# Attention tiles and feed-forward rounds of six layers: two stages per layer, or one stream

## The chip, the core and the metric

The kernel runs on one core of one Trainium2 chip. The metric is the device time of one execution in microseconds (us). Five engines work beside each other and meet at semaphores: TensorE (matmuls and transposes; PE in the profile, its weight loads PEld), VectorE (DVE), ScalarE (ACT), GpSimd (POOL) and SyncE (SP), which starts the transfers. Every engine has its instructions in order in a queue of its own.

## The reference, cut to what matters

64 sequences of 64 tokens, 128 features, in fp32. A cross-attention comes first and a second cross-attention and a mixture of experts come last; between them, and only this is changed, stand six layers of local attention and a gated feed-forward block:

```
for l in range(6):
    x = x + attn(shift_tokens(x), Wqkv[l], Wo[l])      # 16 heads of 64, window 32
    x = x + ffn(shift_tokens(x), W1[l], W2[l])         # 128 -> 2 x 341 -> 128

attn:  q, k, v = split(x @ Wqkv);  q, k = rotary(l2norm(q)), rotary(l2norm(k))
       softmax(8 q k^T, masked) @ v @ Wo
ffn:   xn = layernorm(x) * g + b;  a, gate = split(xn @ W1 + b1)
       (a * gelu(gate)) @ W2 + b2
```

`shift_tokens` moves half of the features by one token, so a tile is read again through a transfer within the core's memory, from `Y` to `xsd` (attention) or `xsf` (feed-forward).

## The kernel before

The residual `Y` holds 32 tiles of 128 tokens (NT). A layer's attention works tile by tile. A feed-forward round takes two tiles, so there are 16 rounds (NF). Every engine runs through the same steps with a body of its own, and the order within the body is written by hand. In a step of the attention (`d_body`) four tiles are in flight: `n` is loaded and turned, `a` is projected (`chunk`, `values`) and gets its rotary embedding (`rope`, the squares and their sums), `b` is turned again (`turn`), gets its scores and the softmax, `c` gets its probabilities turned (`probsT`), the product with the values (`pv`) and the output projection into bank `pp`, which VectorE adds to `Y`. GpSimd sums the rope's halves (`turn_sum`), scales by the inverse norm (`unit`) and the softmax's inverse sum (`probs`). A round (`f_body`) has stages of the same kind: statistics, normalise and turn (`xnT`), three hidden blocks (`hidden`, ScalarE's `gelu`, VectorE's `gated`), and the down product (`f_y`) with its sum.

`stream` (L305 to L319) makes the loop: some steps written out, a loop of two steps, L313, and the last steps written out. It is called twice per layer, with 35 steps for the attention and 19 for the rounds. Around it every engine loops over the layers (L1557 on TensorE, L1117 on VectorE):

```
with pe.Fori(0, DEPTH) as l:
    ...
    stream(pe, NT, d_body, l * NT, l * (NT // 2), 4)
    pe.wait_ge(sem("ffn_loaded"), l * FFN_LOADS + FFN_LOADS)
    ...
    stream(pe, NF, f_body, l * NF, l * (NF // 2), 4)
```

Names used below: turn bank (`pt_`, named turn in the profile), rope on VectorE is L987 and L988, its idle time is seen at L987; L999 is the clamp of the squared norms, L1436 a projection chunk, L1454 a turn of `b`, L1481 of the probabilities, L1511 of the next tile's input, L1495 `pv`, L1524 the output projection; L1535 a hidden block, L1547 the down product; L760 the gelu, L772 the explicit load of the exponential's table; L743 the logarithm of the norms. The last layer's rounds hold two further stages (`e_`, `h`), the norm for the next cross-attention. SyncE's queue issues the tile loads, the round loads and the weights in one order; `past(engine, name, count)` is a wait on a counter.

## Time and profile before

| what | us |
|---|---|
| median of 3 runs | 4562.96 (4555.24 to 4566.67) |
| the profiled execution, its own time | 4562.57 |
| its span, first to last instruction | 4560.5 |
| TensorE busy | 4214.2 (92%) |
| VectorE busy | 3501.8 (77%) |
| GpSimd busy | 2884.7 (63%) |
| ScalarE busy | 2547.9 (56%) |
| first layer's first turn, TensorE | at 687.93 |
| last layer's last down product, TensorE | at 3924.17 |

The mean granted TensorE clock is 0.961 of full speed. The profile is of one execution; "start" is counted from the span's start. Matmuls are pipelined, their ends are modelled, so the distance from one start to the next says more than a duration.

### The profile page before, as it was taken

How to read it: one execution, taken by the hardware profiler on the slowest of the kernel's cores; microseconds unless marked ns; L12 is line 12 of the kernel's file. 1: busy time of each engine (PE TensorE's matmuls, PEld its weight loads, DVE VectorE, ACT ScalarE, POOL GpSimd, SP SyncE). 2: the span in 40 equal slices, each digit the busy share in tenths (PEclk: the TensorE clock that was granted, in tenths of full speed). 3: DMA queues.
4: the chain of work that ended last, by engine and by line, in shares of the span. 5: the costliest groups of instructions: out<-in, count | busy, mean ns of one | idle time of the engine just before them, and what ended most of it. 6: DMA issues, size and time to landing. Idle time of an engine off the chain costs nothing.

```text
span 4560.5 us, 148424 instructions
## 1 busy us (share of the span) xinstructions
PE 4214.2 (92%) x51751; PEld 2907.5 (64%) x51751; DVE 3501.8 (77%) x7368; ACT 2547.9 (56%) x5842; POOL 2884.7 (63%) x3664
## 2 busy tenths in 40 slices
PE   6999998999899988999889998999889998788899
PEld 4777775666666666666656666666666665566655
DVE  4666668997699967999679985999769995577566
ACT  2555555666466655666456663666546664355322
POOL 2333337887288855888378882888648885655300
PEclk9999999999999999999999998999999999887699
DMA  2000010000100010000100001000000000000000
GB/s 83 7 7 7 6 41 6 5 5 6 43 6 5 5 30 20 5 5 6 36 11 5 5 6 43 6 5 5 28 22 5 5 7 11 21 12 12 4 7 11
DMA packets 160438, 64.07 MB, mean 14 GB/s; under 512 B 121365, under 2 KB 155937, under 8 KB 159521
## 3 DMA queue, kind: packets, MB, share of 16 engines
q1 hardware_dynamic: 160288, 62.05, 5.3%
q8 instruction: 98, 1.61, 0.1%
q14 instruction: 52, 0.42, 0.0%
HBM read 26.54 MB, written 2.10 MB: 6 GB/s over the span
## 4 chain that ended last, share of the span: by engine, by line
PE 33%; DVE 29%; issue 25%; POOL 5%; ACT 4%; DVEq 1%; SPq 1%; ACTq 1%; POOLq 0%; DMA 0%
DVE ss L993 6%; DVE big L988 6%; DVE mx L1005 5%; PE pj L1535 3%; DVE big L987 3%; DVE e L1012 3%; DVE qn L987 3%; PE pj L1378 3%; PE turn L1454 3%; PE pp L1336 2%; PE sc L1547 2%; ACT big L698 2%; PE po L1351 2%; PE sc L1697 1%; PE turn L1535 1%
## 5 line engine op out<-in xcount | busy, mean ns | idle before, releaser
L1436 PE MATMUL pj<-wqkv,xcT 128*128 128x512 f32 x1536 | 830.4, 624 | 24.5 <-DVE big L988 9.6
L690 ACT ACTIVATE big<-pj 128x512 f32<-128x512 f32 x768 | 459.1, 598 | 244.3 <-PE pj L1436 176.1
L530 POOL TENSOR_TENSOR big<-big 128x512 f32<-128x512 f32 x384 | 486.0, 1277 | 132.0 <-DVE big L988 132.0
L988 DVE TENSOR_TENSOR big<-pj,ropes 128x512 f32<-128x512 f32 x768 | 522.4, 680 | 0.0
L530 POOL TENSOR_TENSOR qn<-qn,big 128x512 f32<-128x512 f32 x384 | 486.5, 1278 | 35.6 <-DVE big L988 35.6
L993 DVE TENSOR_REDUCE ss<-big 128x8 f32<-128x512 f32 x768 | 504.2, 678 | 0.1
L1524 PEld LDWEIGHTS pp<-wo,oT 128*128 128x128 f32 x3072 | 366.8, 196 | 154.5 <-ACT oT L713 154.1
L525 POOL TENSOR_TENSOR e<-e,rc 128x512 f32<-128x512 f32 x384 | 392.8, 1045 | 46.1 <-DVE rc L1023 46.1
L1524 PE MATMUL pp<-wo,oT 128*128 128x128 f32 x3072 | 403.9, 286 | 7.0 <-ACT oT L713 7.0
L519 POOL TENSOR_TENSOR qn<-qn,ny 128x512 f32<-128x512 f32 x384 | 396.9, 1045 | 7.5
L519 POOL TENSOR_TENSOR big<-big,ny 128x512 f32<-128x512 f32 x384 | 396.8, 1045 | 7.5
L725 ACT ACTIVATE e<-e 128x512 f32<-128x512 f32 x384 | 242.1, 630 | 280.1 <-DVE e L1012 280.1
L1443 PE MATMUL pj<-wqkv,xcT 128*64 128x512 f32 x1536 | 375.5, 606 | 18.1 <-DVE big L988 18.0
L987 DVE TENSOR_TENSOR qn<-pj,ropec 128x512 f32<-128x512 f32 x384 | 262.5, 683 | 105.9 <-PE turn L1454 86.1
L987 DVE TENSOR_TENSOR big<-pj,ropec 128x512 f32<-128x512 f32 x384 | 262.6, 684 | 87.2 <-PE turn L1454 69.9
L1454 PEld LDWEIGHTS turn<-K,qn 128*128 128x128 f32 x1536 | 179.1, 140 | 217.0 <-POOL qn L519 109.8
L1454 PEld LDWEIGHTS turn<-K,big 128*128 128x128 f32 x1536 | 182.0, 141 | 206.9 <-POOL big L519 95.6
L1012 DVE TENSOR_TENSOR e<-sc,mx 128x512 f32<-128x512 f32 x384 | 265.7, 692 | 46.5
L1005 DVE TENSOR_REDUCE mx<-sc 128x8 f32<-128x512 f32 x384 | 260.6, 679 | 44.9 <-PE sc L1470 44.9
L1436 PEld LDWEIGHTS pj<-wqkv,xcT 128*128 128x128 f32 x1536 | 235.1, 193 | 93.0 <-DVE big L988 75.8
L1454 PE MATMUL turn<-K,qn 128*128 128x128 f32 x1536 | 234.2, 275 | 39.5 <-ACT big L698 23.8
L1481 PEld LDWEIGHTS pp<-K,e 128*128 128x128 f32 x1536 | 187.6, 143 | 122.9 <-issue 96.8
(322 smaller groups left out, 9605.8 us busy)
## 6 DMA issues: line engine op xcount, KB each, us to landing
wqkv<-in_L_ffn_Wqkv SPq DMA_DIRECT2D x6, 1536.0 KB, 6.5
xsd<-Y SPq DMA_DIRECT2D x192, 32.0 KB
xsd<-Y SPq DMA_DIRECT2D x384, 15.8 KB
xsf<-Y SPq DMA_DIRECT2D x96, 64.0 KB
xsf<-Y SPq DMA_DIRECT2D x192, 31.5 KB
xsx<-Y SPq DMA_DIRECT2D x64, 64.0 KB, 1.8
xsx<-CT SPq DMA_DIRECT2D x64, 64.0 KB, 1.9
wo<-in_L_ffn_Wo SPq DMA_DIRECT2D x6, 512.0 KB, 7.5
```

Source lines behind the costliest of these rows:

```text
L519: nc.gpsimd.tensor_tensor(uv, uv, bc(ny[:, tile.par, 8 * i:8 * i + 8], DK), ALU.mult).then_inc(sem("d_un"), 1)
L525: nc.gpsimd.tensor_tensor(ev, ev, bc(rc[:, p, 0:8], S), ALU.mult).then_inc(sem("d_pr"), 1)
L530: nc.gpsimd.tensor_tensor(U[a.par][i], U[a.par][i], t2b[i % 2], ALU.add).then_inc(sem("d_add"), 1)
L690: nc.scalar.activation(sqb[i % 2], pj[i % 2][:, :], ACT.Square).then_inc(sem("d_sq"), 1)
L987: nc.vector.tensor_tensor(t1v, pv, cos, ALU.mult)
L988: nc.vector.tensor_tensor(t2v, swapped, sin, ALU.mult).then_inc(sem("d_r"), 1)
L993: nc.vector.tensor_reduce(ss[:, i, :], sqb[i % 2].rearrange("p (h d) -> p h d", d=DK), AX, ALU.add).then_inc(sem("d_ss"), 1)
L1005: nc.vector.tensor_reduce(mx[:, p, 0:8], sv, AX, ALU.max).then_inc(sem("d_mx"), 1)
L1012: nc.vector.tensor_tensor(e[:, p, :].rearrange("p (a t) -> p a t", t=S), sv, bc(mx[:, p, 0:8], S), ALU.subtract).then_inc(sem("d_sub"), 1)
L1436: mm(pj[i % 2][:, :], xcT[:, a.par, :], wqkv[:, i * 512:i * 512 + 512], start=True, stop=True).then_inc(sem("d_ch"), 1)
L1454: last = nc.tensor.transpose(pt_[:, j * P:j * P + P], U[b.par][i][:, j * P:j * P + P], ident)
L1524: last = mm(pp[:, 0:D], oT[:, k, :], wo[:, k, :], start=(k == 0), stop=(k == HP - 1))
```

## The change

All engines go through one list of steps, 192 tiles of all six layers and eight steps behind them, made by `all_layers`. A `Pass` gives the body the tiles `n`, `a`, `b`, `c` and the rounds that are in flight; round r stands two steps for each of its stages, so that one round is begun in every second step. Even steps do the hidden blocks, odd ones the normalisation and, one stage later, the down product. The first eight steps of a layer are written out, the others are a loop of four. The hidden blocks now use the banks `po` of the attention output, the down product uses `pp`, and the turns of `b` use `pt_` and `pp` in turn. The weights of a layer are loaded in parts (`q`, `scales`, `k`, `v`, `o`; `norm`, `up`, `biases`, `down`), each behind the last use of the old part. ScalarE loads the gelu's table and then the exponential's in every even step. Its square of a chunk stands ahead of the first copy; the clamp is now two activations and an identity on it. The last layer's additional norm lies in the last layer's steps. The core of the diff:

```diff
-f_hid = [pj[0], pj[1], pt_]
+f_hid = [po[0], po[1], po[0]]
+f_hidden = sb("f_hidden", [P, 3, FT * P])
+f_xcT = sb("f_xcT", [P, 2, FT * P])
+LAGS, ROUND_LAGS, SEAM = 4, 5, 8
+def all_layers(eng, body):
+tiles, rounds = DEPTH * NT, DEPTH * NF
+def known(k, **more):
+    def one(j, n, m):
+        return Tile(j, j % m, j % 2, j // 2) if 0 <= j < n else None
+    body(Pass([one(k - i, tiles, NT) for i in range(LAGS)], [one(k // 2 - i, rounds, NF) for i in range(ROUND_LAGS)],
+              k % 2, in_po=min(max(k - 3, 0), tiles), **more))
+def moving(l, p, i, **more):
+    def one(j, m, k):
+        return Tile(l * m + j + k * i, (j + k * i) if p < NT else j % m, j % 2, l * (m // 2) + (j // 2) + (k // 2) * i)
+    c = one(p - 3, NT, 4)
+    body(Pass([one(p - q, NT, 4) for q in range(LAGS)], [one(p // 2 - q, NF, 2) for q in range(ROUND_LAGS)],
+              p % 2, in_po=c.g, **more))
+def inside(l, last):
+    with eng.Fori(0, (NT - SEAM) // 4) as i:
+        for p in range(SEAM, SEAM + 4):
+            moving(l, p, i, last=last)
+for k in range(SEAM):
+    known(k, at=k, layer=0)
+with eng.Fori(0, DEPTH - 1) as l:
+    inside(l, False)
+    for p in range(SEAM):
+        moving(l, NT + p, 0, at=p, layer=l + 1)
+inside(DEPTH - 1, True)
+for k in range(tiles, tiles + SEAM):
+    known(k, last=True)
+def attention_weights(l, part):
+    if part == "q":
+        past(sp, "d_ch", l * (4 * NT) - 2)
+        past_waits(sp, "went_on")
+        sp.dma_start(wqkv[:, 0:INNER], Wqkv[l, :, 0:INNER]).then_inc(sem("wq_in"), 16)
+    if part == "k":
+        past(sp, "d_ch", l * (4 * NT))
+        past_waits(sp, "went_on")
+        sp.dma_start(wqkv[:, INNER:2 * INNER], Wqkv[l, :, INNER:2 * INNER]).then_inc(sem("wk_in"), 16)
+    if part == "v":
+        past(sp, "d_vp", l * (2 * NT))
...
+def load_steps(p):
+    if p.at == 0:
+        tile_load(p.n)
+        if isinstance(p.layer, int):
+            for part in ("norm", "up", "biases", "down"):
+                ffn_weights(0, part)
+            past(sp, "x_ch", 6 * NT)
+            for wst, src in ((wst1, w1), (wst3, w3), (wst2, w2)):
+                sp.dma_start(wst, src.rearrange("e i d -> i e d")).then_inc(sem("exp_loaded"), 16)
+        else:
+            for part in ("q", "scales", "k", "v"):
+                attention_weights(p.layer, part)
+    elif p.at == 6 and not isinstance(p.layer, int):
+        ffn_weights(p.layer, "down")
+        tile_load(p.n)
+    else:
+        tile_load(p.n)
+    if not isinstance(p.layer, int):
+        if p.at == 3:
+            attention_weights(p.layer, "o")
+        if p.at == 4:
+            ffn_weights(p.layer, "norm")
+            ffn_weights(p.layer, "up")
+            ffn_weights(p.layer, "biases")
+    if p.odd_round(2):
+        ffn_round(p.odd_round(2).g, p.odd_round(2).t, p.odd_round(2).par)
+all_layers(sp, load_steps)
     unit(b, 1)
     probs(0)
+    unit(b, 2)
...
     turn_sum(0)
+    mean_square(p.odd_round(2))
+    if z:
+        past(pool, "z_x", z.t * 2 + 1)
+        nc.gpsimd.tensor_tensor(X[:, rows, :], Y[:, rows, :], X[:, rows, :], ALU.add).then_inc(sem("z_x"), 1)
     turn_sum(1)
+    inverse_deviation(p.odd_round(2))
+    z = p.odd_round(4) if p.last else None
+    if z:
+        past(pool, "norm_ag", z.t + (NT + 1))
+        rsqrt(0, FT, "norm_nr", z.t * 2 + 2 * NT)
     turn_sum(2)
+    turn_sum(3)
...
+    if r:
+        nc.scalar.preload_act_table_set("gelu_and_others")
+    square(0)
     turned(0)
-    square(0)
+    gelu(0)
     turned(1)
     square(1)
-    probsT(0)
     if n:
         past(act, "d_xT", n.g + 1)
         past(act, "d_vp", n.g * 2 - 2)
         nc.scalar.copy(xcT[:, n.par, :], pt_[:, 0:P]).then_inc(sem("d_xc"), 1)
+    gelu(1)
+    probsT(0)
     square(2)
+    gelu(2)
+    probsT(1)
     turned(2)
-    probsT(1)
     square(3)
     turned(3)
+    if r or p.begins(0):
+        nc.scalar.preload_act_table_set("natural_log_exp_and_others")
     if a:
-        past(act, "d_cl", a.g + 1)
-        nc.scalar.activation(xh[:, :], ssc[:, :], ACT.Ln).then_inc(sem("d_ln"), 1)
+        past(act, "d_ss", a.g * 4 + 4)
+        nc.scalar.activation(xr[:, :], ss[:, :, :].rearrange("p c h -> p (c h)"), ACT.Relu, bias=tiny[:, 1:2]).then_inc(sem("d_cl"), 1)
+        past(act, "d_cl", a.g * 2 + 1)
+        nc.scalar.activation(xh[:, :], xr[:, :], ACT.Ln, bias=tiny[:, 0:1]).then_inc(sem("d_ln"), 1)
+    outT(0)
+    if a:
+        past(act, "d_nt", a.g * 4)
+        nc.scalar.activation(ssc[:, :], xr[:, :], ACT.Identity, bias=tiny[:, 0:1]).then_inc(sem("d_cl"), 1)
         past(act, "d_ln", a.g + 1)
         past(act, "d_un", a.g * 4 - 4)
         nc.scalar.activation(ny[:, a.par, :], xh[:, :], ACT.Exp, scale=-0.5).then_inc(sem("d_rn"), 1)
-    outT(0)
     outT(1)
+    x = p.odd_round(2)
+        nc.scalar.activation(f_xcT[:, x.par, :], pt_[:, 0:2 * P], ACT.Identity, scale=fg[:, 0:1], bias=fg[:, 1:2]).then_inc(sem("f_xT"), 1)
     exps(0)
     values(0)
     exps(1)
     values(1)
+    def gated(j):
+        if h:
+            if j == 0 and p.begins(6):
+                dve.wait_ge(sem("up_in"), p.layer * 112 + 112)
+            m = FBLK[j][1]
+            past(dve, "f_gl", h.g * 3 + (j + 1))
+            if j == 0:
+                past(dve, "f_y", h.g - 1)
+            nc.vector.scalar_tensor_tensor(hT[0:m, h.par, j, :], f_hid[j][0:m, 256:512], fb1[0:m, 0, j:j + 1], f_hidden[0:m, j, :], ALU.add, ALU.mult).then_inc(sem("f_hT"), 1)
     rope(0)
     square_sum(0)
...
+    gated(0)
     rope(1)
...
     square_sum(1)
+    gated(1)
...
     square_sum(2)
+    gated(2)
...
     rope(2)
     square_sum(3)
-    clamp()
     rope(3)
...
+    y = p.odd_round(3)
+    if y:
+        past(dve, "f_y", y.g + 1)
+        ds = bass.ds(y.t * FT, FT)
+        nc.vector.tensor_tensor(Y[:, ds, :], pp[:, 0:2 * D].rearrange("p (a d) -> p a d", a=2), Y[:, ds, :], ALU.add).then_inc(sem("y_ready"), FT)
     row_max(0)
+            if i == 0:
+                past(pe, "d_tc", b.g * 4 - 1)
+                if p.rounds[3] and not p.odd:
+                    past(pe, "f_xT", p.rounds[3].g + 1)
+            elif i == 1:
+                past(pe, "d_res", b.g - 1)
+            elif i == 2:
+                if n:
+                    past(pe, "d_xc", n.g + 1)
+                else:
+                    past(pe, "d_tc", b.g * 4 + 1)
+            elif c:
+                past(pe, "d_pc", c.g * 2 + 2)
             else:
-                past(pe, "d_tc", b.g * 4 + i)
+                past(pe, "d_tc", b.g * 4 + 2)
+            bank = (pt_, pp)[i % 2]
+    def hidden(j):
+        if h:
+            o, m = FBLK[j]
+            if j == 0:
+                past(pe, "f_xT", h.g + 1)
+                if p.begins(6):
+                    pe.wait_ge(sem("up_in"), p.layer * 112 + 112)
+            if j < 2:
+                past(pe, "d_oc", p.in_po * 2 + (j - 1))
+            else:
+                past(pe, "f_hT", h.g * 3 + 1)
+            for k in (1, 0):
+                last = mm(f_hid[j][0:m, (1 - k) * 256:(1 - k) * 256 + 256], fw1[:, k * FI + o:k * FI + o + m], f_xcT[:, h.par, :], start=True, stop=True)
+            last.then_inc(sem("f_h"), 1)
+    chunk(0)
+    hidden(0)
     turn(0)
-    chunk(0)
     turn(1)
     chunk(1)
-    probsT(0)
+    hidden(1)
     if n:
         pe.wait_ge(sem("d_in%d" % n.par), n.half * 48 + 48)
         if b:
-            past(pe, "d_tc", b.g * 4 + 2)
+            past(pe, "d_tc", b.g * 4 + 1)
         else:
             past(pe, "d_xc", n.g)
         nc.tensor.transpose(pt_[:, 0:P], xsd[:, n.par, :], ident).then_inc(sem("d_xT"), 1)
+    probsT(0)
     chunk(2)
     turn(2)
+    hidden(2)
     probsT(1)
     chunk(3)
     turn(3)
     pv()
     scores()
+    if y:
+        past(pe, "f_hT", y.g * 3 + 3)
+        if p.begins(7):
+            pe.wait_ge(sem("fw2_in"), p.layer * 48 + 48)
+        if b:
+            past(pe, "d_tc", b.g * 4 + 4)
+        elif c:
+            past(pe, "d_pc", c.g * 2 + 2)
+        else:
+            past(pe, "d_res", p.in_po)
+            pe.wait_ge(sem("y_ready"), y.g * FT + NT)
+        for i in range(FT):
+            for j, (o, m) in enumerate(FBLK):
+                k = m + (j == 2)
+                last = mm(pp[:, i * D:i * D + D], hT[0:k, y.par, j, i * P:i * P + P], fw2[0:k, j, :], start=(j == 0), stop=(j == 2))
+        last.then_inc(sem("f_y"), 1)
...
     values(0)
+    if x:
...
     values(1)
     if c:
+        if p.begins(3):
+            pe.wait_ge(sem("wo_in"), p.layer * 16 + 16)
         past(pe, "d_oc", c.g * 2 + 2)
+        if b:
+            past(pe, "d_tc", b.g * 4 + 4)
+        else:
+            past(pe, "d_pc", c.g * 2 + 2)
+        if y:
+            pe.wait_ge(sem("y_ready"), y.g * FT + (NT + FT))
         for k in range(HP):
```

## Rows read from the trace of the kernel before

**Rows 1.** Windows by stage: length, busy us (instructions) per engine, clock, DMA.
```profile
741.00:1104.00 363.00, 356.75 (x5057) 231.37 (x5054) 331.70 (x596) 247.89 (x514) 324.40 (x380) 1.00 0.02 5
...
687.90:1143.80 455.90, 431.63 (x5984) 278.16 (x5984) 392.89 (x709) 294.68 (x608) 383.66 (x448) 0.98 0.02 5
1143.80:1224.80 81.00, 72.87 (x416) 59.82 (x416) 47.68 (x177) 34.10 (x66) 14.23 (x32) 0.94 0.21 56
```

**Rows 2.** Timeline of TensorE, steady attention step: start, us, engine, line, operation.
```profile
918.10 1.02 PE L1436 MATMUL pj<-wqkv,xcT 128*128 128x512 f32 x2
919.28 0.63 PE L1454 MATMUL turn<-K,big 128*128 128x128 f32 x4 [0.15 <-ACT big L698]
919.75 1.02 PE L1436 MATMUL pj<-wqkv,xcT 128*128 128x512 f32 x2
920.61 0.60 PE L1481 MATMUL pp<-K,e 128*128 128x128 f32 x4
921.04 0.27 PE L1511 MATMUL turn<-K,xsd 128*128 128x128 f32 x1
921.39 1.13 PE L1436 MATMUL pj<-wqkv,xcT 128*128 128x512 f32 x2
922.35 0.60 PE L1454 MATMUL turn<-K,big 128*128 128x128 f32 x4
...
924.14 0.60 PE L1454 MATMUL turn<-K,big 128*128 128x128 f32 x4
924.67 1.30 PE L1495 MATMUL po<-pT,xo 64*64 64x64 f32 x64
...
929.19 2.05 PE L1524 MATMUL pp<-wo,oT 128*128 128x128 f32 x16
...
931.51 1.02 PE L1436 MATMUL pj<-wqkv,xcT 128*128 128x512 f32 x2
```

**Rows 3.** Timeline of TensorE, one steady feed-forward round.
```profile
1188.00 1.03 PE L1535 MATMUL turn<-kT,fw 128*85 128x256 f32 x4
...
1190.82 1.50 PE L1547 MATMUL sc<-fw,hT 128*128 128x128 f32 x12
...
1192.38 1.02 PE L1535 MATMUL turn<-kT,fw 128*85 128x256 f32 x4
```

**Rows 4.** Groups of instructions, steady attention: busy us, mean ns, idle before.
```profile
L530 POOL TENSOR_TENSOR big<-big 128x512 f32<-128x512 f32 x55 | 69.6, 1277 | 3.7 <-DVE big L988 3.7
...
L999 DVE TENSOR_TENSOR ssc<-ss,tiny 128x32 f32<-128x32 f32 x27 | 20.8, 771 | 0.9
...
L743 ACT ACTIVATE xh<-ssc 128x32 f32<-128x32 f32 x27 | 6.2, 229 | 41.1 <-DVE ssc L999 41.1
```

**Rows 5.** Groups of instructions, steady feed-forward.
```profile
L1060 DVE SCALAR_TENSOR_TENSOR hT<-pj,fb,e 128x256 f32<-128x256 f32 x30 | 13.8, 477 | 2.6 <-ACT e L760 2.5
```

**Rows 6.** Timeline of VectorE, the first rope of a step.
```profile
906.64 0.69 DVE L987 TENSOR_TENSOR big<-pj,ropec 128x512 f32<-128x512 f32 x1 [0.84 <-PE turn L1454]
```

**Rows 7.** Timeline of ScalarE, the two table loads of a layer.
```profile
1150.77 1.28 ACT L760 ACT_TABLE_LOAD   x1 [2.30 <-PE pj L1535]
1152.07 0.90 ACT L760 ACTIVATE e<-pj,fb 128x256 f32<-128x256 f32 x2
...
1219.61 0.47 ACT L760 ACTIVATE e<-turn,fb 85x256 f32<-85x256 f32 x1 [1.73 <-PE turn L1535]
1220.10 1.28 ACT L772 ACT_TABLE_LOAD   x1
```

**Rows 8.** TensorE's branches by source line: layer loop, then step loops (ns min/median/max).
```profile
L1557 PEldq COMPARE_BRANCH  x6: 76/3403/3602, 1220.9 to 3924.3; - x6
...
L313 PEldq COMPARE_BRANCH  x141: 76/208/242, 109.8 to 4267.6; - x141
```

**Rows 9.** Timeline of TensorE, fourth tile's turn and the last down product.
```profile
719.94 0.27 PE L1511 MATMUL turn<-K,xsd 128*128 128x128 f32 x1
...
3924.17 1.60 PE L1547 MATMUL sc<-fw,hT 128*128 128x128 f32 x12 [1.23 <-DVE hT L1060]
```

## What the change does to the time, predicted before its run

> **What bounds the kernel now.** I read the busy shares by stage first. In the steady part of an attention stage TensorE is busy 356.75 of 363 us, VectorE 331.70, GpSimd 324.40, ScalarE 247.89, at a granted clock of 1.00 [rows 1]. A step is 13.41 us long (projection of one tile at 918.10, of the next at 931.51 [rows 2]), so per step VectorE has 12.25 us of work, GpSimd 11.98, ScalarE 9.16. Busy matmuls can hide waits, so I then read the order of TensorE inside one step, start to start [rows 2]. A projection chunk that is not held takes 0.86 (919.75 to 920.61), four transposes 0.43 (920.61 to 921.04). Against that, chunk 0 is followed after 1.18 (0.32 lost: the second turn waits until ScalarE has emptied the only turn bank), the transpose of the next tile's input by 0.35 instead of about 0.11 (0.24 lost, chunk 2 waits for the first rope), chunk 2 takes 0.96 (0.10 lost) and the last turn 0.53 (0.10 lost). That is 0.76 lost, 12.65 of work: TensorE is the bound and little is idle.
>
> A feed-forward round is 4.38 us (1188.00 to 1192.38 [rows 3]), TensorE without a gap: hidden blocks 2.82, down product and turn 1.56. The stage as a whole, 81.0 us [rows 1], is 16 x 4.38 = 70.1 and 10.9 of filling and draining.
>
> The idle time lies at the ends. An attention stage lasts 455.9 us [rows 1]. Its first three steps take 32.0 (687.9 to the fourth tile's turn at 719.94 [rows 9]), then 29 steps of 13.41 are 388.9, and 35.0 are left for the last two and a half steps. With 32 x 13.41 = 429.1 of steady time, 26.8 are ends; with the 10.9 of the feed-forward stage 37.7 per layer, 226 us in six. The last layer's feed-forward stage holds the next stage's statistics besides and is longer; the sum below takes that in by its end.
>
> **The change, part by part.**
>
> *One stream.* There are 192 tiles and 5 + 3 steps behind them, and 96 rounds at one per two steps. Let P be the length of a pair of steps. TensorE's work in a pair is 2 x 12.65 + 4.38 = 29.7 with no wait left; with the waits of now it is 2 x 13.41 + 4.38 = 31.2. Both ends go into the range. The other engines in a pair: VectorE 24.5, less two clamps of 0.77 [rows 4], plus 47.68 / 16 = 2.98 of a round = 25.9; ScalarE 18.3 + 34.10 / 16 = 2.13 + two table loads of 1.28 (under 0.1 of which the round already holds) + four activations on 32 columns of 0.23 = 23.8; GpSimd 24.0 + 0.89 = 24.9 [rows 1, 4, 7]. None reaches 29.7, so the bound stays TensorE as long as no chain through two or three engines is longer.
>
> *Order and banks.* Turns alternate between two banks, which takes away the 0.32. Chunk 0 comes before turn 0, and its square before ScalarE's first copy. VectorE now sits idle 0.84 before its first rope [rows 6], because that square is behind a copy; the first rope comes earlier by up to about this, and the 0.24 ahead of chunk 2 and its own 0.10 can go. In the even step a hidden block lies between chunk 0 and turn 0 and covers GpSimd's last scaling too. The clamp leaves VectorE (0.77 [rows 4]) for two more small activations on ScalarE. GpSimd's fourth sum moves ahead of the Newton step, so turn 0's operand comes later by 1.28 [rows 4]; chunk 0 (0.86) and in even steps hidden 0 (a third of 2.82) now lie ahead of that turn, so I count nothing in even steps and up to 0.4 in odd ones.
>
> *Table loads.* A load takes 1.28 (from 1150.77), starts 0.02 behind the activation before it (1219.61 + 0.47, load at 1220.10), and the gelu starts 0.02 behind it [rows 7]. Two of them stand in each even step. The first lies where ScalarE ends the tile before and TensorE does chunk 0 and hidden 0 (0.86 + 0.94), so it is nearly hidden; it costs between 0 and 1.28. The second lies between the last turn's copy and the copies of the attention output, which the output projection waits for. TensorE has the product with the values, the scores and the values' projection to do meanwhile (4.5 us, 924.67 to 929.19 [rows 2]), so I leave 0.3 of it on the path; the bounds are again 0 and 1.28.
>
> The Trainium skill, "ScalarE: Activation LUTs", section "What ACT_TABLE_LOAD costs", adds a drain of 1.38 us to every switch. The trace shows no such gap on either side of the load. By that rule P would be up to 2.8 longer, 33.1, and the time about 4565; what rows give for it is rival E.
>
> *P.* Best 29.7; I give back 0.3 for the second load and 0.3 for GpSimd's later scaling and the first load together: P = 30.3.
>
> *Start and end.* From 687.9 the first three steps stay 32.0; steps 3 and 4 have no round work, 26.8; steps 5 to 191 are 93.5 pairs; the rest of step 192, then 193 and 194, are the 35.0 of now plus two hidden groups and one down group, 2 x 2.82 + 1.56, 42.2. Then the last round runs alone: the latency of a round is the 10.9 of the stage's ends plus one period of 4.4; its input is now loaded only when the last tile is done, about 2 more (estimate), 17.4 in all. Together 806.3 + 93.5 P. The statistics for the next stage lie inside the stream; behind the last down product comes what comes now.
>
> *Seams.* Five times the layer's weights change in mid stream. SyncE's queue is in order: the value weights wait for the last values of the old layer, and behind them stand the second tile's input and a round's input; chunk 2 needs the value part as well as the key part. I count 2 us for that, 0 to 5. The loop over layers still jumps back five times: TensorE's jump takes 3.4 us (L1557), against 0.2 for a loop over steps (L313) [rows 8]. That jump is in the 37.7 of now and comes back here with 3.4. Five seams of 5.4 are 27.
>
> *Sum.* The last down product starts at 3924.17 and ends at 3925.8 [rows 9]. New: 806.3 + 93.5 x 30.3 + 27 = 3666.4. That is 259.4 earlier; against the profiled execution's 4562.57 us (span 4560.5) it gives 4303, and the median of the three runs, 4562.96, is only 0.4 away. I say 4300.
>
> **The rivals.**
>
> *A. The waits stay* (P = 31.2). For: every step now has 0.76 of waits although each engine has slack, so a ring through ScalarE and VectorE sets them, and ScalarE gets 5.5 us more per pair. Against: the two largest have named causes that the new order removes. 806.3 + 2917.2 + 27 = 3750.5, so 4387.
>
> *B. The loop over steps becomes a far jump.* It goes from two steps to four. TensorE issues 187 matmuls and 187 weight loads a step (5057 in 27 steps [rows 1]) and some 20 queue instructions (estimate); four steps with two rounds are about 1700 instructions. The jump over a layer, about 3600, costs 3.4 us; the jump over two steps, about 800, costs 0.2 [rows 8]. 1700 lies between. There are 30 such jumps (six rounds in six layers, the last of each not taken): 30 x 3.4, less what TensorE's queue covers, is 75 to 102; with 87 it gives 4390.
>
> The Trainium skill, "Runtime: NRT & Kernel Launch", section "Instruction fetch mechanics", gives TensorE room for 2048 instructions and a fetch for a taken branch that leaves it. By that the new loop fits, narrowly, and B costs nothing; a whole layer does not fit, and there the trace agrees.
>
> *C. All waits go* (P = 29.7): 4247. It needs both table loads hidden and is not likely.
>
> *D. Slower: ScalarE's additions stand in series with its waits.* Place: the even step. ScalarE waits 4.2 of 13.41 us now for partners. If those waits stay and loads, gelus and small activations (2.56 + 1.42 + 0.45) are added behind them, the even step is 17.8, and the odd one 13.41 + 1.56 + 0.45 = 15.4, P = 33.3, 4584. The deciding point is P = (3925.8 - 833.3) / 93.5 = 33.1. For: hidden 2 waits for the first gated block, and the probabilities' product waits for the last, so matmul, gelu and gate follow each other twice in the step. Against: three hidden blocks give ScalarE and VectorE 2.8 us of TensorE time to use, and one gelu takes 0.47, one gated block 0.48 [rows 5, 7].
>
> *E. The table loads stand on the path in full.* A load finds ScalarE idle in most places now; behind a busy engine it could cost twice its 1.28. Two in a pair, 2.56 beyond the 0.6 that I count: P = 32.9, 4547. Against it speaks the load at 1220.10, which follows a gelu at once [rows 7]. The Trainium skill's drain, above, is this rival.
>
> *F. It doesn't overlap.* A round could run as an island, if a barrier held the tiles. The waits in the step are per tile and round, none on a whole layer, so this gets no chance of its own.
>
> **How the numbers follow.** Forecast 0.50; A 0.20; B 0.16; C 0.06; D 0.04; E 0.04, half of it so far that nothing measurable is left. The range for 8 in 10 goes from between C and below it (waits under 0.76 may be uncounted) to above A and B, with a small part of both together: 4210 to 4430. A change of 0.3%, 14 us, is about what a measurement of this kernel can tell. Faster is all but D and half of E, 0.94; within 0.02; slower 0.04.
>
> **What the changed profile would show.** The granted clock stays 1.00 from the fourth step to the last tile, and the forty slices show no dips between layers. Starts of chunk 0 two steps apart give P: 30.3 if I am right, 31.2 for A. A branch of 3.4 us on the step loop's line is B. Turn 1 follows turn 0 by 0.43 without waiting for a copy; VectorE's idle time before the first rope falls below 0.84. VectorE's share rises towards 85% and ScalarE's to 78% in the steady part. Around each layer change at most 6 us are lost. I am wrong if TensorE waits over 1.5 us per pair for ScalarE's output copies (A or D), if the seams take over 10 us each, or if TensorE is not the engine with the least idle time.

## The result, and the profile after

| | us | ratio to before, 95% interval |
|---|---|---|
| before, median of 4 runs beside the new kernel | 4561.01 | |
| after, median of 4 runs | 4435.03 (4433.17 to 4438.25) | 0.9725 (0.9708 to 0.9741) |
| forecast | 4300, 4210 to 4430 | |

The change makes the kernel faster by 126 us, where I had forecast 260. The measured time lies 5 us above my range.

Page of the kernel after: the engines' busy time, the queue that brings instructions (packets, MB, share), and the chain that ended last.

```profile
PE 4164.6 (94%) x51751; PEld 2901.7 (65%) x51751; DVE 3525.9 (80%) x7208; ACT 2841.5 (64%) x6406; POOL 2869.7 (65%) x3633
...
q8 instruction: 393, 6.44, 0.6%
...
PE 77%; DVE 9%; issue 8%; POOL 3%; ACT 1%; SPq 1%; DVEq 0%; ACTq 0%; POOLq 0%; DMA 0%
```

TensorE is still the bound, but 8% of the chain is "issue": TensorE waited for nothing that the profile shows. The instruction queue moved 393 packets; in the kernel before it had moved 98 (1.61 MB).

The stretch that answers to the steady window of [rows 1], with the same columns:

```profile
757.00:1192.00 435.00, 420.70 (x5414) 285.82 (x5413) 372.94 (x719) 321.36 (x655) 338.00 (x407) 0.99 0.06 14
```

TensorE is idle in 14.3 of 435 us although the two kinds of work are interleaved now. Where those are is seen at the turn of the next tile's input, one per step. Timeline of TensorE, kernel after:

```profile
822.54 0.27 PE L1649 MATMUL turn<-K,xsd 128*128 128x128 f32 x1
...
836.17 0.27 PE L1649 MATMUL turn<-K,xsd 128*128 128x128 f32 x1
...
847.20 2.05 PE L1697 MATMUL pp<-wo,oT 128*128 128x128 f32 x16
851.25 1.12 PE L1542 MATMUL pj<-wqkv,xcT 128*128 128x512 f32 x2 [2.00 <-issue]
...
855.67 0.27 PE L1649 MATMUL turn<-K,xsd 128*128 128x128 f32 x1
```

From one such turn to the next is 13.63 us in every second step (822.54 to 836.17) and 16.80 in the others where nothing disturbs it, a pair 30.43. From 836.17 to 855.67 it is 19.50: 2.00 idle ahead of chunk 0 at 851.25. That idle time comes once in four steps, at the loop's end. Branches of TensorE's sequencer by source line (ns, min/median/max): the loop over steps (L360) and over layers (L366).

```profile
L360 PEldq COMPARE_BRANCH  x36: 83/3626/3983, 847.3 to 3752.5; - x36
```
```profile
L366 PEldq COMPARE_BRANCH  x5: 79/3532/3732, 1299.8 to 3377.2; - x5
```

Each of these lines also counts the last pass, where the branch is not taken (83 and 79 ns): of the 36 on L360 30 are taken, of the 5 on L366 four. In [rows 8] the loops over two steps had 208 ns. The other engines' branches on L360 have medians of 45 to 56 ns. Now the loop's end, on TensorE alone, costs as much as a layer's.

I added up, over the 186 distances from the sixth tile's turn (744.56) to the last one's (3741.69), what each is above 16.80 or 13.63. The sum is 167.1 us:

| place | us |
|---|---|
| end of the 4-step loop and the step behind (27 of 30 branches slow) | 110.8 |
| layer jump and the step behind (4, 18.6), and the same two steps in the first and the last layer (1.7) | 20.3 |
| first three steps of a layer, the seam (5) | 32.8 |
| exit of the 4-step loop, all else | 3.2 |

The 27 are all 25 in layers 0 to 4 and two of the last layer's five.

A part of this is TensorE's clock. Behind some of the gaps it falls to its lower level, 1.2 GHz. Timeline of TensorE at the loop's next end, then windows behind three gaps (2.00, 2.21 and, at the seam below, 3.36 us idle), with the columns of [rows 1]:

```profile
915.61 1.67 PE L1542 MATMUL pj<-wqkv,xcT 128*128 128x512 f32 x2 [2.21 <-issue]
```
```profile
851.25:854.65 3.40, 3.40 (x16) 2.45 (x17) 1.36 (x3) 1.47 (x4) 1.95 (x2) 1.00 0.02 5
916.10:919.40 3.30, 3.30 (x9) 2.17 (x8) 1.20 (x2) 0.60 (x1) 1.69 (x2) 0.50 0.02 5
1195.95:1199.35 3.40, 3.40 (x11) 2.26 (x11) 3.40 (x11) 0.60 (x1) 1.11 (x1) 0.50 0.11 24
```

The step of a slow loop end is 2.4 to 3.0 us too long where the clock stays at 1.00 (18 of the 27) and 4.1 to 4.6 where it falls (9). It also falls in the step of the tables at all five seams, and behind three of the four layer jumps. In the whole stream 64.8 us stand at 0.50, so up to 32 of the 167.1 us (estimate, half of that) are the price of the clock behind a gap and not of the gap itself.

The seam. Timelines of the kernel after, first TensorE, then VectorE, then GpSimd:

```profile
1191.53 0.31 PE L1649 MATMUL turn<-K,xsd 128*128 128x128 f32 x1
1191.78 0.63 PE L1601 MATMUL pp<-K,e 128*128 128x128 f32 x4
1195.76 1.94 PE L1542 MATMUL pj<-wqkv,xcT 128*128 128x512 f32 x2 [3.36 <-DVE big L1108]
```
```profile
1190.41 0.39 DVE L1088 SCALAR_TENSOR_TENSOR ropec<-K,qs 128x64 f32<-128x64 f32 x1 [0.16 <-issue]
1190.72 1.05 DVE L1089 SCALAR_TENSOR_TENSOR ropes<-K,qs 128x32 f32<-128x32 f32 x1
1191.68 1.08 DVE L1090 SCALAR_TENSOR_TENSOR ropes<-K,qs 128x32 f32<-128x32 f32 x1
1192.69 1.11 DVE L1088 SCALAR_TENSOR_TENSOR ropec<-K,qs 128x64 f32<-128x64 f32 x1
1193.72 0.18 DVE L1089 SCALAR_TENSOR_TENSOR ropes<-K,qs 128x32 f32<-128x32 f32 x1
1193.82 0.18 DVE L1090 SCALAR_TENSOR_TENSOR ropes<-K,qs 128x32 f32<-128x32 f32 x1
1194.42 0.69 DVE L1107 TENSOR_TENSOR big<-pj,ropec 128x512 f32<-128x512 f32 x1 [0.42 <-DVE ropes L1090]
```
```profile
1189.67 1.05 POOL L627 TENSOR_TENSOR e<-e,rc 128x512 f32<-128x512 f32 x1
1190.67 1.04 POOL L621 TENSOR_TENSOR qn<-qn,ny 128x512 f32<-128x512 f32 x1
1191.67 1.05 POOL L627 TENSOR_TENSOR e<-e,rc 128x512 f32<-128x512 f32 x1
1192.67 1.04 POOL L621 TENSOR_TENSOR qn<-qn,ny 128x512 f32<-128x512 f32 x1
```

Before the first rope of a new layer VectorE builds six small tables, 3.6 us in a row. TensorE's chunk 2 waits 3.36 for the rope behind them, and the chunk then takes 1.94 instead of 1.02, at the granted clock of 0.50 shown above. The old kernel has the same six instructions, but at the start of a layer, where the pipeline was filling anyway. I had not priced them.

ScalarE's two table loads, groups of the kernel after (busy us, mean ns, idle before):

```profile
L858 ACT ACT_TABLE_LOAD x97 | 124.5, 1283 | 1.7
L839 ACT ACT_TABLE_LOAD x96 | 123.2, 1283 | 8.9 <-issue 7.3
```

193 loads with 10.6 us of idle time ahead of them in all: there is no drain on entering a load. Behind it there is none either: the median distance from a load's end to the next activation's start is 0.01 us.

The end of the stream, and the first turn of the last part:

```profile
3741.69 0.27 PE L1649 MATMUL turn<-K,xsd 128*128 128x128 f32 x1
...
3808.46 1.60 PE L1673 MATMUL pp<-fw,hT 128*128 128x128 f32 x12 [1.07 <-DVE hT L1148]
...
3818.24 0.41 PE L1734 MATMUL pj<-K,xsx 128*128 128x128 f32 x2 [0.30 <-ACT egT L947]
```

The last down product ends at 3810.06, before at 3925.77 [rows 9]: 115.7 earlier. The span is 4431.3, so 621.2 follow, where 634.7 followed before; those 13.5 make the 129.2 by which the span is shorter.

### The profile page after: what moved, and what is told of

Its sections match the earlier page's. It is cut to its first block, busy times and chain, and to the rows that moved or that the text cites. A ratio compares the mean times of both kernels' runs of the same rounds, so it can differ in the third digit from the quotient of the medians.

```text
span 4431.3 us, 147857 instructions
## 1 busy us (share of the span) xinstructions
PE 4164.6 (94%) x51751; PEld 2901.7 (65%) x51751; DVE 3525.9 (80%) x7208; ACT 2841.5 (64%) x6406; POOL 2869.7 (65%) x3633
## 4 chain that ended last, share of the span: by engine, by line
PE 77%; DVE 9%; issue 8%; POOL 3%; ACT 1%; SPq 1%; DVEq 0%; ACTq 0%; POOLq 0%; DMA 0%
PE pj L1542 13%; PE pp L1697 7%; PE pj L1549 7%; PE po L1634 6%; PE po L1617 4%; PE sc L1588 4%; PE pp L1572 4%; PE turn L1572 3%; PE pp L1601 3%; PE pj L1480 3%; PE pp L1438 2%; PE pp L1673 2%; DVE big L1108 2%; PE po L1453 2%; PE sc L1832 2%
## 5 line engine op out<-in xcount | busy, mean ns | idle before, releaser
L1542 PE MATMUL pj<-wqkv,xcT 128*128 128x512 f32 x1536 | 817.2, 614 | 86.9 <-issue 66.3
L1114 DVE TENSOR_REDUCE ss<-big 128x8 f32<-128x512 f32 x768 | 515.5, 672 | 4.4 <-ACT big L793 4.4
L1697 PEld LDWEIGHTS pp<-wo,oT 128*128 128x128 f32 x3072 | 357.3, 191 | 156.1 <-issue 109.4
L1549 PE MATMUL pj<-wqkv,xcT 128*64 128x512 f32 x1536 | 394.4, 613 | 1.3 <-DVE big L1108 1.3
L1697 PE MATMUL pp<-wo,oT 128*128 128x128 f32 x3072 | 393.9, 281 | 1.6 <-ACT oT L816 1.2
L1634 PE MATMUL po<-f_xcT,fw 128*128 128x256 f32 (+1 forms) x1152 | 307.0, 391 | 1.5 <-DVE hT L1148 0.8
L1634 PEld LDWEIGHTS po<-f_xcT,fw 128*128 128x128 f32 (+1 forms) x1152 | 208.1, 185 | 121.2 <-issue 95.4
L1588 PE MATMUL sc<-kT,big 64*64 64x64 f32 x12288 | 234.2, 222 | 27.2 <-issue 27.1
L1132 DVE TENSOR_REDUCE sm<-e 128x8 f32<-128x512 f32 x384 | 259.4, 676 | 0.0
```

The costliest lines, as they stand in the source:

```text
L1114: nc.vector.tensor_reduce(ss[:, i, :], sqb[i % 2].rearrange("p (h d) -> p h d", d=DK), AX, ALU.add).then_inc(sem("d_ss"), 1)
L1542: mm(pj[i % 2][:, :], xcT[:, a.par, :], wqkv[:, i * 512:i * 512 + 512], start=True, stop=True).then_inc(sem("d_ch"), 1)
L1549: last = mm(pj[bb][a2 * 64:a2 * 64 + 64, :].rearrange("p (q c) -> p q c", c=2 * DK), xcT[:, a.par, bb * 64:bb * 64 + 64], wv[:, a2], start ...
L1588: last = mm(sc[q, c0:c0 + S], qT[r, hp, q], kT[r, hp, q], start=False, stop=True, skip_group_check=True)
L1634: last = mm(f_hid[j][0:m, (1 - k) * 256:(1 - k) * 256 + 256], fw1[:, k * FI + o:k * FI + o + m], f_xcT[:, h.par, :], start=True, stop=True)
L1697: last = mm(pp[:, 0:D], oT[:, k, :], wo[:, k, :], start=(k == 0), stop=(k == HP - 1))
```

## The experiments

Theory T1: TensorE's backward branch of the 4-step loop has to fetch its target again, because the loop (1701 instructions by my count of the generated ones and by the profile's records from one branch to the next, against 792 for two steps before) with what is fetched ahead needs more room than there is. T2: the loop's end costs that for another reason (register work, waits that meet, the other engines' loops, the clock). S1 and S2 are the two theories of the seam: the build of the tables lies on the path, or the weights arrive late. A slow branch is one of over 3 us; "increments" are idle semaphore instructions that only move the code behind them. Four runs stand behind each median up to e8, five behind e9, one behind e10 to e14, so these five have no interval; e1 to e4, e5 to e8, e9 to e11 and e12 to e14 ran together, each group beside the kernel before (4556.5, 4562.6, 4558.1, 4565.1 us).

| run | us | ratio to before (95%) | slow branches of 30 |
|---|---|---|---|
| e1 | 4357.8 | 0.9568 (0.9547 to 0.9590) | 8 |
| e2 | 4420.8 | 0.9700 (0.9677 to 0.9723) | 30 |
| e3 | 4337.9 | 0.9522 (0.9495 to 0.9550) | no loop |
| e4 | 4413.3 | 0.9695 (0.9668 to 0.9721) | 27 |
| e5 | 4413.3 | 0.9677 (0.9649 to 0.9705) | 27 |
| e6 | 4346.0 | 0.9526 (0.9499 to 0.9552) | no loop |
| e7 | 4323.6 | 0.9484 (0.9460 to 0.9507) | 0 |
| e8 | 4324.8 | 0.9496 (0.9470 to 0.9522) | no loop |
| e9 | 4309.5 | 0.9453 (0.9430 to 0.9476) | 0 |
| e10 | 4332.3 | | 0 |
| e11 | 4339.6 | | 5 |
| e12 | 4442.3 | | 30 |
| e13 | 4370.1 | | 5 |
| e14 | 4292.2 | | 0 |

**Padding, e1 and e2.** The only edit, in TensorE's program ahead of its first wait for data:

```
+            for _ in range(190):            # e2: 40
+                past_waits(pe, "went_on")
             pe.wait_ge(s_ld, NLOAD)
```

> 190 idle semaphore increments are put into TensorE's program at its very start, where it waits for the first loads; nothing else changes. Counted in instructions of 64 bytes, TensorE's 4-step loop is 1701 long, or 6.6 blocks of 256 instructions (the instruction queue moves 16 KB at a time). In the changed kernel it lies over 8 such blocks in layers 0 to 4 (22.4 to 29.1), where each of the 25 backward branches measured 3.6 us, and over 7 in the last layer (42.35 to 49.0), where only 2 of 5 did. The padding moves both loops to start just behind a block's edge (23.2 to 29.8 and 43.1 to 49.7), 7 blocks each. Theory T1 (the backward branch has to fetch its target again because the loop with the block fetched ahead needs more room than there is): the slow branches go in all six layers, or in 3 of 5 as in the last: 60 to 110 us less, 4325 to 4375 us. Rival T2 (the 3.6 us is the price of the loop's end itself: register work, waits that meet there, other engines' loops, the clock): the place of the code can't matter, 4430 to 4440 us. The padding's own cost is nothing under either.

> The same padding with 40 increments: the loop of layers 0 to 4 stays over 8 blocks (22.6 to 29.2), the last layer's, so far over 7, now lies over 8 (42.5 to 49.2). T1: the last layer's five branches all become slow, three more than before, each about 4 us with the step after it: 10 to 16 us more, 4445 to 4451 us. T2: 4430 to 4440 us.

Branches of the 4-step loop, first of e1, then of e2; and the instruction queue of each:

```profile
L360 PEldq COMPARE_BRANCH  x36: 76/222/4023, 843.5 to 3667.4; - x36
```
```profile
L360 PEldq COMPARE_BRANCH  x36: 83/3388/3928, 849.2 to 3742.5; - x36
```
```profile
q8 instruction: 223, 3.65, 0.3%
```
```profile
q8 instruction: 420, 6.88, 0.6%
```

The same instructions at another place take 77 us less. The median branch falls from 3626 to 222 ns and 170 fewer packets of instructions are moved. T2, by which the place doesn't matter, is out, and the clock with it: it falls behind a gap and is not what makes the gap. e2 came as T1 says in number (the last layer's five are all slow), but not in time: 14 us less, not 10 to 16 more. Its 30 slow ends cost 107.0 with the steps behind, 3.6 each, where the 27 before cost 4.1 each; the step behind is longer by 1.0 on average in the kernel after, and in e2 only in the last layer, by 0.8. Why it is longer stays open. So the price of a slow jump moves with the place too, and I had taken it for fixed.

**TensorE's loops written out, e3 and e6.** e3 replaces the loop over steps, e6 all loops of the stream, on TensorE alone (`for i in range(6)` for `Fori`; in e6 one `for k in range(200)` over `known`).

> TensorE alone has the loop over steps written out inside each layer (its loop over the layers, and every other engine's loops, stay). T1: all 30 backward branches of the 4-step loop are gone and with them 104 to 111 us: 4324 to 4340 us; the instruction queue still moves at least as many blocks, since the code streams. T2 in the form 'it is the other engines' or DMA's part of the loop's end, or the clock': 4425 to 4440 us, with the gaps at the same steps.

> TensorE's whole stream is written out, the loop over layers too: no backward branch of either loop is left on TensorE (the other engines keep theirs). Against the kernel with the inner loop alone written out (4337.9 us) T1 says that the 5 layer jumps go with what they measured there, 9.6 + 4.3 us: 4320 to 4327 us. T2 (at the layer's edge it is something else that meets, not the jump): no change, 4335 to 4340 us. What is left above the clean pair of 30.43 us then is the seams (27 us) and gaps of 0.6 to 1.2 us where straight code reaches a new block.

e3 confirms the size of the term: 97 us less. e6 missed. The layer jump did go, from 13.9 to 9.1 with its step, but the time is not shorter. Its excess over clean steps is 77.1 us: 30.6 at the seams, and 46.5 in gaps, most of them of 0.6 to 1.4, spread over the whole stream. Its instruction queue:

```profile
q8 instruction: 333, 5.46, 0.5%
```

By my count TensorE's program is 84,300 instructions there, 253 per packet. In the looped kernels that are placed well, the steps inside the loop have no such gap from its second pass on. That the gaps are late packets was not tested by itself.

**The seam, e4 and e5.** e4 builds the keys' three tables ahead of `rope(2)` instead of ahead of `rope(0)`; e5 builds tables in layer 0 alone:

```
                 square_sum(2)
                 gated(2)
+                if p.begins(1):
+                    table(1)          # e4: L1088 to L1090 for the keys
                 rope(2)
```

> In the first step of a layer DVE builds six small rotary tables in one go ahead of the first rope (L1088 to L1090, 1190.41 to 1194.0 at the first seam, three of them at 1.05 to 1.11 us), and TensorE's chunk 2 then waits 3.36 us for DVE. Here the three tables of the keys are built behind square_sum(2), just ahead of rope(2). Theory S1 (a seam costs 6.5 us because the table build lies on the path): half of the build moves into DVE's slack, 1.5 to 4 us less at each of 5 seams: 4415 to 4428 us. Theory S2 (it is the weights, which arrive late by the order of SyncE's waits): 4433 to 4437 us.

> The six rotary tables are built in layer 0 alone, and the other five layers go on with layer 0's (their scales are still loaded; what is computed in layers 1 to 5 is thereby another function of the same shape). The seam's excess in the changed kernel's trace is 27.9 us in the step of the build and 4.5 in the one behind. S1: nearly all of it is the build: 22 to 30 us less, 4405 to 4413 us, and chunk 2's wait for DVE of 3.4 us is gone. S2 (something of the weights is late as well): no more than half of it goes, 4420 to 4435 us.

The first three steps of a layer lost 32.8 us in the kernel after, 16.1 in e4, 7.8 in e5. That is S1: about 25 of the 33 us go with the table build, over half of that is hidden by spreading it, and the weights' arrival explains little. The 25 hold the lower clock behind the wait too: none of e5's table steps has a stretch at 0.50, two of e4's five have one, all five in the kernel after. Both medians are 22 us under that of the kernel after, e4's 2 us below its range for S1 and e5's at the edge of its own, so the times don't tell e4 from e5; and e4's interval overlaps with that of the kernel after. For e4 it is the trace that shows it.

**Where the fast places are, e7 and e10 to e13.** The same padding with other counts; e7 has e4's tables as well.

> All loops as in the changed kernel, 168 increments of padding at TensorE's start, and the tables built in two halves. The loops then start 22 and 2 instructions behind a block's edge and end at .73 and .65 of their seventh block; with 190 they started at 44 and 24, ended at .82 and .74, and about 8 of 25 branches in layers 0 to 4 were still slow, none of 5 in the last. If a slow branch comes from the block that is fetched ahead while the loop's last block runs, an earlier end leaves fewer: 0 to 4 slow branches, 8 to 16 us less than the 4357.8 us with 190; the halves of the tables give 12 to 16 more, as alone (5 x 2.6 and the step behind): 4327 to 4340 us. If the end's place in its block doesn't matter: as many slow ones, 4341 to 4347 us.

> 148 increments of padding: the loop of layers 0 to 4 starts 2 instructions behind a block's edge (7 blocks), the last layer's starts 18 before one (8 blocks). T1: all 25 branches of layers 0 to 4 are fast (about 0.2 us), all 5 of the last layer slow (3.4 to 3.9 us): 4435 less about 105 and plus about 12, 4335 to 4348 us. T2 (the slow ones belong to the layers or the time, not to the place): the last layer's stay fast.

> 232 increments: both loops over 7 blocks, but they end at .98 and .90 of the last one. If only the count of blocks matters: all fast, as with 168: 4335 to 4340 us. If the fetch ahead from the loop's last block takes the room (T1's finer form, after 8 of 25 slow at an end of .82 and 2 of 5 at .996): at least 10 of the 30 are slow again, most in layers 0 to 4: 4370 to 4420 us.

> 70 increments: by the count of instructions the loops start at 180 (layers 0 to 4) and 160 (last layer) of a block's 256, and lie over 8 blocks. Slow branches so far by that start: 238, 2, 22, 24, 66: none; 44, 86, 90: some (8 of 25, 5 of 25, 2 of 5); 110, 130, 150: all. Strict T1 (it is the number of blocks touched, and the count is off by a few dozen at most): 180 and 160 are slow, all 30: 4415 to 4430 us. T2 (place decides nothing, the earlier ones were chance): 30 branches anywhere.

> 100 increments: starts at 210 and 190. A loop of 1701 instructions touches 7 blocks for 91 of the 256 places and 8 for the other 165. 238 was fast and 150 slow: if the fast places are 91 in a row that end near 70, they begin near 235, and 210 and 190 are slow: 4415 to 4430 us, all 30. If they are fast, more places fit than 7 blocks explain, and the room is larger than that: about 4335 us.

Branches of the 4-step loop and the instruction queue of e7; then the branches of e12; then those of e13 in layers 0 to 4, and in the last layer:

```profile
L360 PEldq COMPARE_BRANCH  x36: 76/215/246, 848.2 to 3637.6; - x36
```
```profile
q8 instruction: 147, 2.41, 0.2%
```
```profile
L360 PEldq COMPARE_BRANCH  x36: 82/3514/3970, 846.3 to 3761.9; - x36
```
```profile
L360 PEldq COMPARE_BRANCH  x30: 76/215/230, 848.0 to 3143.9; - x30
```
```profile
L360 PEldq COMPARE_BRANCH  x5: 83/3489/3593, 3404.5 to 3677.3; - x5
```

By where the loop starts within 256 instructions (my count): 210, 238, 2, 22, 24 and 66 have no slow branch; 44, 86 and 90 have 8 of 25, 5 of 25 and 2 of 5; 110, 130, 150, 160, 180 and 190 are slow always. Of the fast ones 238, 24 and 66 rest on the five branches of one last layer each. e13 has both kinds in one run: one loop at 210 and its copy at 190. In e7 not one of the 30 is slow and 147 of 393 packets are left.

The packets say what a slow branch does. Above the 147 of e7 the kernel after moves 246 more for 27 slow branches, e2 273 for 30, e12 274 for 30 (421 in all), e13 44 for 5 (191): 9 each. That is the whole loop, 7 or 8 blocks of 256, and one or two more.

Not all came as expected. e7 lies 3 us below its range. In e10 the last layer stayed fast, as its T2 has it; e13, where the last layer alone is slow, shows that it is the place all the same. e11 has 5 slow branches, where none or at least 10 were expected, e12 all 30 but 12 us more than its range. In e12 15 of the 30 slow ends have the lower clock behind them, in e13 all five, for 6.8 us each, and these five cost 7.1 us each.

What fell is the strict form of T1. A loop of 1701 touches 7 blocks from 92 places only, and the six fast places, with one mixed one among them (44), span 113; by the count e10's last layer and e13's layers 0 to 4 lie over 8 blocks, and they were fast. The end's place in the last block doesn't order the mixed ones either.

**A shorter loop at a slow place, e14.**

```
-                        for hp in range(HP):
+                        for hp in range(HP - 2):      # and 192 increments ahead
```

This kernel leaves out the scores of two of the eight head columns.

> The other way to fewer blocks: a shorter loop at the same place. The scores of two of eight head columns are left out in every step of the six layers (those columns keep the band mask alone), which takes 128 of the loop's 1701 instructions: 6.1 blocks; the padding keeps its start at 110 in layers 0 to 4, where with 1701 all 25 branches were slow, and it now touches 7. The work left out is worth 16 of 64 score products a tile, 192 x 0.30 us = 59 us by their busy time. T1: the branches turn fast as well, some 110 us more: 4260 to 4285 us and a branch median near 0.2 us. T2 (the place itself or the loop's end is slow): 4365 to 4385 us, and 3.4 to 3.6 us a branch.

```profile
L360 PEldq COMPARE_BRANCH  x36: 76/208/246, 848.6 to 3600.4; - x36
```

With 1573 instructions the start at 110 has no slow branch, where 1701 had 25 of 25. The time is 7 us above T1's range and 73 below T2's. A distance between turns is only about 0.2 us shorter than before, so the products left out were worth less than their busy time. Place and length both decide, which speaks for room; how much there is, and what is fetched ahead, no run tells.

**Both finds together, e8 and e9.** e8 is e6 with the tables of the queries built behind `rope(3)` of the step before and those of the keys ahead of `rope(2)`; e9 has TensorE looped, 168 increments of padding and the same tables, which is e7 with the early ones.

> TensorE written out altogether, and the tables of the queries built at the end of the step before (behind rope 3 of the last tile), those of the keys ahead of rope(2). Both causes together: 104 to 111 us for the 4-step loop less about 15 for block edges in straight code, 14 to 20 for the layer loop, 16 to 25 for the tables: 4296 to 4312 us. If the early tables only push the softmax that stands behind them and TensorE waits for that instead, the seams keep 12 us: 4308 to 4316 us.

> Both finds together with the least code: 168 increments of padding at TensorE's start, and the rotary tables of the queries at the end of the step before, those of the keys ahead of rope(2). With 168 and the halved tables the run gave 4323.6 us, its seams 15.4 us above the clean steps; the early tables left 4.4 + 3.3 us in the written-out kernel: 5 to 9 us less, 4314 to 4319 us. If the fetch of the looped code and the seams are not independent (a slow branch comes back): 4320 to 4328 us.

VectorE in e9 around the first seam (the six table instructions), and the steady window again:

```profile
1160.68 1.27 DVE L1085 SCALAR_TENSOR_TENSOR ropec<-K,qs 128x64 f32<-128x64 f32 x1 [0.17 <-DVE big L1105]
1161.87 0.24 DVE L1086 SCALAR_TENSOR_TENSOR ropes<-K,qs 128x32 f32<-128x32 f32 x1
1162.04 0.18 DVE L1087 SCALAR_TENSOR_TENSOR ropes<-K,qs 128x32 f32<-128x32 f32 x1
...
1172.24 0.22 DVE L1085 SCALAR_TENSOR_TENSOR ropec<-K,qs 128x64 f32<-128x64 f32 x1
1172.37 0.18 DVE L1086 SCALAR_TENSOR_TENSOR ropes<-K,qs 128x32 f32<-128x32 f32 x1
1172.48 0.18 DVE L1087 SCALAR_TENSOR_TENSOR ropes<-K,qs 128x32 f32<-128x32 f32 x1
```
```profile
757.00:1192.00 435.00, 433.17 (x5722) 295.73 (x5724) 390.98 (x760) 334.34 (x682) 351.75 (x423) 1.00 0.05 13
```

The seams fall to 7.0 us, TensorE is busy 433.2 of the 435 us, and the excess of the stream is 39.4 instead of 167.1: 16.0 layer jumps, 7.0 seams, the rest in the straight part of each layer and the loop's first pass. e9 is the fastest of all with the whole computation: 4309.5, 5.5% under the kernel before, 2.8% under the change. It lies 4.5 us below the range expected, and its five runs lie far apart (4294.9 to 4320.3). Part of that is not the edit: the sixth tile's turn comes at 740.4 in e9's trace, as in e1's and e3's (740.1, 738.7), and at 744 to 750 in the other traces. Against e7 the 14 us are within the intervals. e8 missed its range by 13 us for e6's reason: its steps outside the seams hold 45.4 us of gaps.

## Why the prediction was wrong

The sum was 806.3 + 93.5 P + 27 for the end of the last down product, 3666.4. It came at 3810.1, 143.7 later. Term by term:

| term | forecast | measured | difference |
|---|---|---|---|
| B, end of the 4-step loop, 30 times | 0 in the sum (87 as a rival) | 110.8 | +110.8 |
| seams, 5 x 2 | 10 | 32.8 | +22.8 |
| layer jumps, 5 x 3.4 (only 4 are taken) | 17 | 20.3 | +3.3 |
| P | 30.3 | 30.43 | +12.1 |
| first five steps | 58.8 | 56.7 | -2.1 |
| last turn to the end | 74.8 | 68.4 | -6.4 |
| loop exits, rest | 0 | 3.2 | +3.2 |

Behind the last down product 13.5 us less than "what comes now".

**The step that failed is rival B.** I had the right row: a branch of 3.4 us for a layer, 0.2 for two steps [rows 8], and 1700 instructions between them. I gave the far jump a chance of 0.16, and its 87 us stayed out of the sum. It was the truth of 27 of 30 branches. The sum with B in it is 4390, and with the 110.8 measured 4414, in my range; the seams took it out. B's own bounds, 75 to 102, were too low as well: I priced the branch alone, and the step behind it, longer by 1.0, and the lower clock behind nine of them came on top. From the rows alone a chance near one half was due, and the range should have gone above B together with another miss. The lengths were read badly too. By the profile's records the layer that the jump of 3.4 us goes back over is 2734 instructions long, not about 3600, and the same trace has a loop of 1184 instructions in the first cross-attention whose branch takes 0.2: 1701 lies between these two.

What kept me on the near side was a figure of the Trainium skill: "Runtime: NRT & Kernel Launch", section "Instruction fetch mechanics", gives TensorE room for 2048 instructions. By it 1701 cost nothing. Measured: 1701 fetched again always at six places of fifteen, never at six, sometimes at three. The figure may well be the size of the room; it is not the size of a loop that is safe in it.

**The seams.** I looked for the price in SyncE's queue and the weights (2 us each, 0 to 5) and overlooked what VectorE does at a layer's start. It was 6.6 each, outside my bound, and e5 shows that 5.0 of it goes with the table build, the lower clock behind TensorE's wait included. The step moved these six instructions out of a filling pipeline into a full one. By the rule that every instruction of a moved step counts, they should have been in the list.

**What held.** P: 30.43 measured, 30.3 forecast, from 2 x 12.65 + 4.38 and 0.6 given back. Steps without round work now take 12.86 (729.11 to 741.97) instead of 13.41, so the order and the banks gave 0.55 of the 0.76 that I had found. That 30.43 is so near 30.3 is in part luck: of the 0.6 given back for the table loads and GpSimd's later scaling no run took one part by itself. Rival A (31.2), C (29.7), D (33.3) and E (32.9) are all out by the clean pair. For E and D the table loads decide: 1283 ns each, 10.6 us idle ahead of all 193, and the next activation right behind. The drain of 1.38 us per switch that the Trainium skill gives ("ScalarE: Activation LUTs", "What ACT_TABLE_LOAD costs") does not show in this trace. F, no overlap, is out as well. "At most 6 us around each layer change" was wrong: 6.6 at the seam and 4.7 at the jump with the step behind it are 11.3, past the 10 that I had named as the sign of an error. The clock is 0.99 in the steady window, not quite the 1.00 I named: it falls to 0.50 behind two of the gaps, and e9 without them has 1.00.

**The last part.** 13.5 us less behind the last down product: from its end to the first turn of the last part 8.2 against 6.6, from the first turn to the last 315.0 against 325.8 (4133.25 and 4258.13 for the last), behind that 298.1 against 302.4. The code of these steps is the same. About 3.3 of the 10.8 is one step of 14.1 us in the kernel before, where TensorE's clock was granted at 0.50, its lower level of 1.2 GHz; the kernel before:

```profile
4102.00:4113.00 11.00, 11.00 (x81) 8.41 (x81) 7.62 (x19) 3.70 (x9) 4.68 (x10) 0.50 0.04 12
```

Steps of about 14 us come in some traces and not in others (two in e7's last part, none in e1's). The whole stretch from first to last turn, before and after, shows the same on a larger scale:

```profile
3932.32:4258.13 325.81, 269.63 (x3124) 204.53 (x3124) 231.45 (x594) 165.02 (x378) 185.02 (x322) 0.83 0.04 12
```
```profile
3818.24:4133.25 315.01, 260.47 (x3123) 197.89 (x3124) 231.91 (x595) 164.30 (x377) 183.16 (x318) 0.86 0.04 13
```

With the same matmuls TensorE stood 112.6 us at the lower level before and 87.2 after. Half of the difference, 12.7 us (estimate), is enough for all of the 10.8, and it differs from one trace to the next, so these microseconds can't be put down to the change. 5.4 of the 10.8 lie in the first two steps (2.2 and 8.2 against 6.0 and 9.8), which I did not follow further.

## What to carry to other kernels

When a loop's body grows, treat the backward branch as a term of the sum, with the price of the farthest branch in the trace until the new length is measured; a median of 3 us on its line, or an instruction queue that moves far more packets than before (here 393 against 98), shows that it has happened. Then try moving the loop by a few dozen idle instructions before writing it out: here the placed loop's trace has fewer gaps than the straight code's, which pays small ones all along. The place has to be found again after every edit that changes the code ahead of the loop. And price a gap with the clock behind it: here a gap of 2 to 3.4 us was followed in many places by 3.4 us or more at half the clock. And when stages are merged, list what every engine does once at the old stage's start, since the fill that hid it is gone.

## What the runs showed of the hardware that I had not expected

A small VectorE instruction with all operands in SBUF can be held until GpSimd's running instruction ends. In the seam above three table instructions took 1.05 to 1.11 us and ended at 1191.77, 1192.76 and 1193.80, and GpSimd's ended at 1191.71, 1192.72 and 1193.71; the same instructions behind that took 0.18. In e9 the one beside a busy GpSimd took 1.27 and the later ones 0.18 to 0.24. The normalisation of a round shows the same; groups and timeline of the kernel after, VectorE, then GpSimd:

```profile
L1190 DVE TENSOR_SCALAR fxn<-xsf,dif,rstd 128x128 f32<-128x128 f32 x192 | 168.8, 919 | 2.2 <-POOL rstd L643 2.2
```
```profile
877.53 1.84 DVE L1190 TENSOR_SCALAR fxn<-xsf,dif,rstd 128x128 f32<-128x128 f32 x2
```
```profile
876.78 2.51 POOL L632 TENSOR_TENSOR big<-big 128x512 f32<-128x512 f32 x2
```

It averages 919 ns, where the old kernel, with GpSimd mostly idle in the rounds (14.23 of 81 us, [rows 1]), had 349 (L1051 there). Instructions of VectorE that read PSUM (the rope, 0.68) are not stretched, nor are its sums over a tile in SBUF (L1114, at most 0.69 in 768), so it is not every instruction that stays in SBUF. That the two engines share something is my reading of these times; no run tested it alone.
